# Attention in nine stages of two batches instead of five rounds of four, with stacks and transfers a stage ahead of their scores

## What is computed

```python
x = x + xattn(layernorm(x), ctx, ctx, mask, Wq, Wk, Wv, Wo)   # 16 heads: softmax(Q K^T / sqrt(8)) V, then Wo
x = x + ffn(layernorm(x), wg, w1, w3, w2)
# ffn: logits = x @ wg.T; the two best of 8 experts, weights by softmax over the two
#      y_e = (silu(x @ w1[e].T) * (x @ w3[e].T)) @ w2[e].T;  out = sum over the two of weight * y_e
```

## Time and profile before

| | |
|---|---|
| median of three runs (lowest, highest) | 294.29 us (292.64, 297.12) |
| the profiled execution: its time, its span | 292.38 us, 290.6 us |
| busy: PE, VectorE (DVE), ScalarE (ACT), GpSimd (POOL) | 211.9, 211.0, 137.2, 91.6 us |
| mean granted TensorE clock, as a share of full speed | 0.819 |
| the chain of work that ended last: PE, DVE, transfers, issue | 39%, 29%, 14%, 8% of the span |

### The profile page before, as it was taken

One profiled execution on the slowest core, in us unless ns is written; L12 is line 12 of the kernel. 1 busy time (PEld: TensorE's weight loads), 2 busy tenths in 40 slices (PEclk: granted clock), 3 DMA queues, 4 the chain that ended last, 5 costly groups with the idle time before them and its releaser, 6 DMA issues.

```text
span 290.6 us, 5041 instructions
## 1 busy us (share of the span) xinstructions
PE 211.9 (73%) x1381; PEld 154.3 (53%) x1381; DVE 211.0 (73%) x618; ACT 137.2 (47%) x293; POOL 91.6 (32%) x104
## 2 busy tenths in 40 slices
PE   0767897898959978769654867677959999988010
PEld 0543564566636555547432644366848899877010
DVE  4689956598737978389778776548897888867095
ACT  5799138364735548234215665324434555544000
POOL 4311200040003010101545366211546564656740
PEclk9995559799978999595965685559999999999655
DMA  6934402332052111320315511240242232221537
GB/s 216 340 103 107 114 11 52 74 90 59 9 117 64 41 29 37 83 59 1 89 48 169 173 39 46 57 101 0 54 101 67 76 91 68 80 76 34 166 82 218
DMA packets 24793, 24.99 MB, mean 86 GB/s; under 512 B 3806, under 2 KB 19168, under 8 KB 24382
## 3 DMA queue, kind: packets, MB, share of 16 engines
q1 hardware_dynamic: 21502, 18.37, 25.2%
q0 software_dynamic: 2688, 5.48, 5.8%
q10 hardware_dynamic: 576, 0.82, 0.9%
HBM read 12.31 MB, written 6.31 MB: 64 GB/s over the span
## 4 chain that ended last, share of the span: by engine, by line
PE 39%; DVE 29%; DMA 14%; issue 8%; ACT 5%; SPq 3%; POOL 1%; POOLq 0%; DVEq 0%; ACTq 0%
DVE m_neg L1405 6%; DMA ys<-big 5%; PE bank L545 5%; PE bank L669 4%; DMA bd<-st 4%; PE bank L704 4%; PE bank L690 4%; PE bank L551 3%; PE bank L769 3%; DMA big<-ys 2%; DVE st L1349 2%; PE bank L743 2%; SPq L434 2%; PE bank L575 2%; PE bank L770 2%
## 5 line engine op out<-in xcount | busy, mean ns | idle before, releaser
L1405 DVE TENSOR_REDUCE m_neg<-bank 128x4 f32<-128x512 f32 x64 | 43.4, 684 | 22.2 <-PE bank L704 22.1
L1047 POOL DMA_INDIRECT ys<-big x39 | 38.1, 976 | 37.9 <-DVE big L1441 23.0
L932 ACT ACTIVATE big<-bank 128x512 f32<-128x512 f32 x64 | 37.3, 597 | 26.3 <-PE bank L690 25.5
L704 PE MATMUL bank<-bd,st 128*128 128x512 f32 x64 | 32.9, 544 | 11.5 <-DMA bd<-st 11.0
L690 PE MATMUL bank<-bd,st 128*128 128x512 f32 x64 | 33.9, 550 | 4.9 <-ACT big L932 3.3
L1013 POOL DMA_INDIRECT xg<-rows,rows_i x24 | 24.1, 1004 | 33.3 <-DVE rows_i L1214 14.2
L997 POOL TENSOR_SCALAR ve<-mv 128x4 f32<-128x4 f32 x8 | 1.8, 226 | 100.8 <-DVE mv L1076 100.8
L807 ACT ACTIVATE st<-bank 128x128 fp32r<-128x128 f32 (+1 forms) x78 | 22.3, 329 | 21.5 <-PE bank L756 15.7
L1349 DVE SCALAR_TENSOR_TENSOR st<-st_hi,cst,bank 128x512 fp32r<-128x512 f32 x32 | 22.9, 747 | 10.4 <-ACT st_hi L904 10.4
L769 PE MATMUL bank<-bd,st 128*128 x78 | 22.9, 315 | 8.8 <-DVE big L1441 8.7
L904 ACT ACTIVATE st_hi<-bank,cst 128x512 fp32r<-128x512 f32 x32 | 21.8, 690 | 10.2 <-PE bank L545 9.9
(11 more groups left out here) (169 smaller groups left out, 467.0 us busy)
## 6 DMA issues: line engine op xcount, KB each, us to landing
bd<-st SPq DMA_DIRECT2D x62, 104.0 KB
big<-xg SPq DMA_DIRECT2D x39, 64.5 KB, 1.8
raw<-in_L_ffn_w SPq DMA_DIRECT2D x2, 1024.0 KB, 7.0
x_all<-in_x SPq DMA_DIRECT2D x4, 256.0 KB, 4.2
rows<-in_mask_BxS_if POOLq DMA_DIRECT2D x4, 256.0 KB, 5.1
ctx_all<-in_L_ffn_w SPq DMA_DIRECT2D x1, 1024.0 KB, 4.9
ctx_all<-in_ctx SPq DMA_DIRECT2D x3, 256.0 KB, 4.8
raw<-ys SPq DMA_DIRECT2D x3, 256.0 KB, 4.6
```

The costliest lines, as they stand in the source:

```text
L704: nc.tensor.matmul(s1[k % s1_ring(u)][:, :].rearrange("p (j q) -> p j q", j=NJ), st[:, u % 2, 0, b - 1, g, :], bd_slot(1, n)[:, g, :, :], ...
L932: nc.scalar.activation(prob[n % 2][:, NJ * g:NJ * (g + 1), :].rearrange("p h q -> p (h q)"), s2[k % 2][:, :], ACT.Exp, scale=SCALE).then_i ...
L1047: pool.indirect_dma_start(ys, bass.IndirectOffsetOnAxis(xt[n % XR][:, D:RW].bitcast(I32), 0), y_sb[n % YR], None, bounds_check=PAIRS - 1, ...
L1405: nc.vector.tensor_reduce(m_neg[:, H * (b - 1) + g:H * b:NG], s1[k % s1_ring(u)][:, :].rearrange("p (j q) -> p j q", j=NJ), X, ALU.max, ne ...
```

## The change

Stages p = 0 to 8 of two batches each replace the rounds. In stage p stand first a *head*: the stacks of stage p+1 (four units: keys of groups 0 and 1, keys of 2 and 3, queries of 0 and 1, queries of 2 and 3, each unit one bank with two groups of two batches, so 256 columns a matmul), between them the transpose of the maxima of stage p-1 and the ends of the two batches of stage p-2. Then come 11 ticks: in tick t the score by query t of stage p (t < 8) and the score by key t-3 of stage p-1. `st` holds four stages, and the diagonals of keys for stage p+1 and of queries for stage p are issued during stage p. The clearing of `va[1]` goes from VectorE to GpSimd. Routing and weight work is placed by stage and tick. All four maxima groups of a batch are unchanged, and so are the transfers' shapes and their number.

```diff
-            for u in range(NQ + 1):
-                front(u)
-                for b in range(QB + 1):
-                    for g in range(NG):
...
+            def stack_unit(p, k):
+                is_k, h = UNITS[k]
+                o = claim(("st", p, k))
+                if k >= 2 and p >= 2:
+                    pe.wait_ge(max_done, 2 * NG * (p - 1))
...
+                for i in range(2):
+                    g = 2 * h + i
...
+            def scores_by_query(p, i):
+                if i < 2:
+                    if p + 1 < NP:
+                        taken(pe, ("st", p + 1, 2 + i))
...
+                if k >= 2:
+                    pe.wait_ge(max_done, k - 1)
...
+            for p in range(NP + 1):
+                front, tail = p + 1 < NP, p >= 2
+                n = 2 * (p - 2)
+                if front:
+                    stack_unit(p + 1, 0)
+                if p >= 1:
+                    transpose_maxima(p - 1)
+                if tail:
+                    heads_by_query(n)
+                if front:
+                    stack_unit(p + 1, 1)
+                if tail:
+                    values(n + 1)
+                    heads_by_dim(n)
+                if front:
+                    stack_unit(p + 1, 2)
+                if tail:
+                    project_out(n)
+                if front:
+                    stack_unit(p + 1, 3)
+                if tail:
+                    heads_by_query(n + 1)
+                for t in range(TICKS):
+                    if t < 2 * NG and p < NP:
+                        scores_by_query(p, t)
+                    if t == 1 and tail:
+                        heads_by_dim(n + 1)
+                    if t >= LEAD and p >= 1:
+                        scores_by_key(p - 1, t - LEAD)
+                    if t == 3 and tail:
+                        project_out(n + 1)
+                    if t == 8 and p >= 1:
+                        values(2 * (p - 1))
+                    for name in fills(p, t):
...
+            for p in range(NP + 1):
...
+                if front:
+                    take_stacks(p + 1, 0)
+                if p >= 1:
+                    take_maxima(p - 1)
+                if tail:
+                    normalise_heads(n)
+                if front:
+                    take_stacks(p + 1, 1)
+                    take_stacks(p + 1, 2)
+                if tail:
+                    take_projection(n)
+                if front:
+                    take_stacks(p + 1, 3)
+                if tail:
+                    normalise_heads(n + 1)
+                for t in range(TICKS):
+                    if p < NP and t < 2 * NG:
+                        largest(p, t)
+                    if p < NP and t == 2 * NG - 1:
...
+                        round_maxima()
+                    if t == 3 and tail:
+                        take_projection(n + 1)
+                    if p in (0, 2, 4):
+                        next_quartet(p // 2 + 1, t)
...
+                    if p in (5, 6) and t in (5, 6, 7):
+                        routing_step(p - 5, t - 5)
...
+                    if p == 7 and t == 4:
+                        second_statistics(2)
```

656 lines of the change are left out of this document (312 added, 344 removed), and 3 rows, old and new, of the table FILLS.

## The result

The changed kernel takes **301.54 us** (median of 4 runs, 299.90 to 303.29) against 293.47 for the kernel before beside it (291.54 to 297.12): a ratio of **1.030, interval 1.020 to 1.040, slower**. The forecast was 293, no change, in a range of 282 to 304. The time lies in the range, near its upper end; the side was wrong.

A forecast was written before the change was run, and what follows sets the result against it. Bound: VectorE in attention, idled by PE's 11.0 us of diagonal waits, then the chain of sends behind quartet 2's statistics. Span 290.6 + 3.7 - 1.0 - 2.1 = 291.2, plus 1.8 around it: 293 us, range 282 to 304.

The forecast's parts named there:

- the clock term: Stages 2 and 4: lower PE clock in tail and next head, bounded by 0 and 4.3 us each, taken as 2.0.
- signs of being wrong: Heads under 6 us, clock under 0.75 in stages 2 to 6, or first tile at a distance the sends do not give.
- the exchange: Turns of attention: 11.0 us of waits for diagonals go; a head, 7.75 us to first maximum, replaces them in every stage.
- The rival of shorter heads: Stage heads lie between VectorE's 4.3 us of work and 7.75; kernel 282 to 287 us; chance 0.30.
- the rival in which load and matmul take turns: Heads: a weight load's 0.19 us more per matmul, 28 in seven heads, 37 us; kernel 330 us; chance 0.01.
- The rival of late transfers: SyncE's ten transfers a stage come late despite the lead, bringing back up to 11 us; kernel 304 us; chance 0.02.
- lower clock in every stage: Rival: PE stays at 1.2 GHz from tick to head, stages 1 to 6 paying 4.3 us each; kernel 307 us; chance 0.21.
- half hidden: Stages 5 and 6: a routing of 4.5 us each, half running on behind the last maximum, holding the next head by 2.2.
- 34.3 us from statistics to first tile: Behind quartet 2's statistics: quartet 1's sends take 15.4 us, quartet 2's then find rows ready; 34.3 instead of 35.3.
- over 75%: Sign expected in stages 2 to 7: VectorE busy over 75% of the time.

The follow-up runs named there:

- after: The changed kernel as first profiled, against the kernel before: that execution took 299.90 us; median of its first runs 301.54 us, ratio 1.030.
- the repeat of after: The changed kernel run again unchanged, on another chip, for a second profile: 303.63 us (2 runs).
- both moves: The changed kernel with the tanh moved into the next head and quartet 2's statistics right behind the last projection: 295.88 us (10 runs), 1.004; its repeat 296.62.
- Experiment 4: The changed kernel with four routing operations of 0.46 us done twice in stages 5 and 6: 306.06 us, 1.044 to the kernel before.
- experiment 3: The changed kernel with quartet 2's statistics right behind the last projection, stage 7's weight pieces later: 301.36 us; instead, quartet 2's tokens transposed at stage 7's end: 301.85.
- the mended kernel: The changed kernel with tanh, statistics and clearings moved, and quartet 2's normalisation, transposes and router ahead of stage 8's weight pieces: 292.64 us, 0.998 to the kernel before.

## Why the prediction was right and where it was wrong

The sum missed the span by 6.9 us (298.1 for 291.2): 4.0 up to quartet 2's statistics (160.04 for 156.0), 3.4 from there to the first tile (37.7 for 34.3), and -0.5 behind it (-2.6 for -2.1). Three steps failed, each answered below: the clock term, a wait of the old lists that the change moved to the turns, and the rows taken to be ready behind the sends. Two of its signs of being wrong came: a clock under 0.75 (stage 2), and a first tile at another distance from the statistics.

**Right: the exchange.** The wait is gone and a head stands in its place. PE is free of stage 2's last score by key at 70.7 and stage 3's first maximum starts at 78.39: 7.7 us, for 7.75 in the sum.

```profile
70.72 0.28 PE L541 MATMUL bank<-ck_hi,ws_hi 128*128 128x256 f32 x1
...
78.39 1.28 DVE L1383 TENSOR_REDUCE m_neg<-bank 128x4 f32<-128x512 f32 x2
```

It is not only the total: PE turns the first heads 1.4 us into the head (1.45 in the sum), begins the values at 2.7 (2.65) and `heads_by_dim` at 3.7 (3.75). The rival of shorter heads did not come. Stages 2 and 3, 19.82 and 15.16 us from first maximum to first maximum, make 35.0 us, for 34.7 (20.4 + 14.3) and against 34.10 before: no gain from the pair, as the text said. Products of 256 columns start 0.12 us apart, as taken from the earlier trace rows:

```profile
130.78 0.28 PE L541 MATMUL bank<-x_lo,ws_hi 128*128 128x256 f32 x1
130.90 0.29 PE L541 MATMUL bank<-x_hi,ws_lo 128*128 128x256 f32 x1
```

That disposes of the rival in which load and matmul take turns; the rule of the Trainium skill, "TensorE: Matmul & The Clock Gate", section on packing small matmuls, from which it came, is not what these rows show in the form in which the prediction cites it; the same section also names a load into the background weight buffer as one that is pulled ahead of running matmuls. The rival of late transfers fell with the missing wait.

**Right up to stage 5, by offsets.** Stage 5's first maximum was forecast at 112.85 and came at 112.01. Within that the start was 1.7 late, stage 4 was 1.9 short, so the agreement is partly luck.

**Wrong: the clock, given only to stages 2 and 4.** The sum put 2.0 us on each and nothing on any later stage. (The price was read from rows in rounds 1 and 2, not in the three rounds that it names.) Stage 2 paid about 1.15 (19.81 at 0.74, against 18.7 at 0.91 in six other profiled runs); stage 4 ran at full clock and paid nothing; stage 5 paid, with no term in the sum. In stages 2 and 4 the mean clock is no price by itself: over the runs that keep these stages they take 18.7 us at 0.82, 0.91 and 1.00 alike, and 19.8 to 19.9 at 0.74. In stage 5 it is: four profiled runs with the tanh out of the way give 18.40 at 1.00, 19.36 at 0.91, 20.64 at 0.83 and 21.63 at 0.76. From these I estimate 1.3 us for each 0.1 and so 21.4 at the 0.77 of after; after's 22.35 is then 3 us of clock and 1 of tanh. At full clock the 18.7 of the sum would have held. The rival "lower clock in every stage" named a right cause but the wrong place and extent: four of its six stages ran at full clock, and the coldest, stage 7, lay outside them.

**Wrong: the link that I left out, ScalarE's tanh at the turn.** From stage 5's first maximum to stage 7's the sum has 36.6 us, the trace 41.35; from there to the statistics it was right (6.55 and 6.68). I let the routing hold the next head by 2.2 us through VectorE alone. There is a second way by which it holds the head: ScalarE's tanh waits for the routing's last step, and the last exponential and the copy of the heads stand behind it. At the end of stage 6 that costs PE 1.7 us of standing (2.07 less 0.40), after which stage 7 runs at 0.54, in the repeat at 0.67. Moving the tanh gives stage 7 2.5 us in both executions, and at one clock in stages 5 and 6 the way of 41.35 is 41.39 in the repeat of after and 35.24 with both moves. The sum looked only at waits that the change adds; this one is old, and the change moved it to where PE has nothing else to do.

**Wrong without a price: the routing "half hidden".** Experiment 4 shows that added routing is not hidden at all. But this did not cost the sum its 4.75 us: the routing measured 4.4 for the 4.5 taken, 1.7 behind the last maximum for the 2.2, and with the tanh moved and stage 5 at full clock the two stages take 36.14, less than the 36.6. What the routing cost more, the rest of the stages cost less.

**Wrong: 34.3 us from statistics to first tile.** The step took the sends of quartet 1 to decide and the rows to be ready behind them. The sends of quartet 1 took 15.1 us, for 15.4, but then those of quartet 2 wait for the rows (first send, GpSimd), which is nearly all of the 3.4:

```profile
181.57 0.97 POOL L1053 DMA_INDIRECT xg<-st_hi,rows_i  x1 [3.17 <-DVE rows_i L1252]
```

The rows come 13 us behind the `mT` of stage 8, whose head is late with everything ahead of it; experiment 3 shows that earlier statistics do not bring them. In the earlier trace rows the wait for rows could be seen already: 1.48 us at 170.62. (That send's source, `rows`, is that of quartet 1's others; the sends from `st_hi` begin at 171.90, so its reading as the first of quartet 2 is doubtful.) What was right is the last part: from rows to first tile 17.18 us, 17.59 before, 16.74 in the mended kernel: the eight sends decide it.

**Mostly wrong: VectorE "over 75%"** was 0.70 to 0.75 in stages 2 to 5, 0.87 in stage 6 and 0.66 in stage 7 up to the statistics.

So the 8 us come back with the order of a few instructions, and with the lists mended the stages cost what the rounds cost. Whether the kernel before would gain from lists mended in the same way was not run, so that the stages are as good as the rounds with equal care is not shown. Of what the mended kernel wins up to `rows_i(2)`, most is the tanh and the statistics: from stage 5's `mT` to these rows after takes 73.4 us, the repeat of both moves 65.7 and the mended kernel 63.8, the last two at 0.91 in stage 5.

What stays open is why stage 5 was granted 0.77 or 0.78 in after and in five of the experiments that leave the tanh ahead of the head. The tanh of stage 5 does not decide it: it comes at 127.13, and PE's products run at the lower level from 114.71 until about 124.5. The same product of the run with the tanh moved, at 113.10, is at full clock:

```profile
114.71 0.80 PE L681 MATMUL bank<-bd,st 128*128 128x512 f32 x1
```

```profile
113.10 0.50 PE L681 MATMUL bank<-bd,st 128*128 128x512 f32 x1
```

Nor do the other runs follow the place of the tanh: stage 5 had 0.76 in the first profile with tanh and statistics moved, and 0.92 in the repeat of after.

## What to carry to other kernels

When work is cut into stages, look at each turn for short instructions that wait in an in-order list, and ask what stands behind them: a tanh of 0.23 us held the head of a stage, which then ran at the lower clock. Give a moment its time by the list that issues the work, not by when its data are ready. And price a lower clock for every stage, from rows of that same work at both levels, rather than for those that look idle: here a clock just over 0.8 was free in one stage and cost over 2 us in another.

## What the runs showed of the hardware

- The granted clock of a stage differs between executions of the same code: stage 5 of the kernel with the tanh moved was 18.40 us at 1.00 and 20.64 at 0.83; two medians of it were 295.78 and 300.45. A difference of 2% between single runs says nothing here.
- What a clock costs differs by stage: stages 2 and 4 took 18.7 us at 0.82, 0.91 and 1.00 and 19.8 to 19.9 at 0.74; stage 5, by my estimate from its four rows above, grew by 1.3 us with each 0.1.
- A higher mean clock bought with added products is not time: 0.84 to 0.89 left the time where it was, 0.82 to 0.90 cost 7.6 us.
- PE's standing of 3.6 us at one turn was followed by a stage at 0.54; with 0.9 us at the same turn the stage had 0.93, in both executions. In the repeat of after it was again 3.6 us and 0.67.
- SyncE takes 8.0 us to issue a stage's eight diagonal transfers, about 1 us each; the trace does not hold their landings. The lead of a stage covers both, since PE waits for none. The queue of SyncE in after, stage 4:

```profile
90.29 8.04 SPq L430 DMA_DIRECT2D bd<-st  x8
```
